# Attention: negated row maxima become rows of the query stack by two DMAs through HBM instead of by TensorE, the ring of banks and VectorE

## The reference, cut to what matters

```python
scores = jnp.einsum('bhqd,bhkd->bhqk', Q, K) * scale
attn = jax.nn.softmax(scores, axis=-1)
out = jnp.einsum('bhqk,bhkd->bhqd', attn, V)
```

## Time and profile before

| | us |
|---|---|
| median of 3 runs | 2127.63 (2123.89 to 2129.58) |
| the profiled execution | 2127.73 |
| its span in the trace | 2125.9 |
| attention in it, first scores to last | 132.79 to some 904 |
| PE busy in the span | 1809.8 (85%) |
| DVE busy | 1201.9 (57%) |
| ACT busy | 905.9 (43%) |
| POOL busy | 436.5 (21%) |
| mean granted clock of TensorE | 0.927 |

### The profile page before, as it was taken

The page is one execution under the profiler, slowest core; times in us unless marked ns, Lnnn a source line. Parts: engine busy times, 40 slices in busy tenths (PEclk is TensorE's granted clock), DMA queues, the critical chain, the costliest instruction groups (busy, mean ns, idle before and its releaser), DMA issues. The chain is left out here.

```text
span 2125.9 us, 37885 instructions
## 1 busy us (share of the span) xinstructions
PE 1809.8 (85%) x11264; PEld 1147.6 (54%) x11265; DVE 1201.9 (57%) x2635; ACT 905.9 (43%) x1362; POOL 436.5 (21%) x570
## 2 busy tenths in 40 slices
PE   7889999999999999976599999999994885067771
PEld 4423444444444444363488888888884465036551
DVE  4578888888888888644611111111113896946334
ACT  3436666666666666743033223323331520031333
POOL 2210000000000000030033333333331001202772
PEclk9969999999999999997799999999997998575996
DMA  4511111111111111054343433444442001141224
GB/s 146 187 42 35 31 34 33 30 37 30 33 34 30 37 30 32 14 166 169 138 109 95 114 113 100 107 116 112 97 112 81 1 1 60 64 158 23 48 40 161
DMA packets 103320, 159.38 MB, mean 75 GB/s; under 512 B 20704, under 2 KB 79392, under 8 KB 97760
## 3 DMA queue, kind: packets, MB, share of 16 engines
q1 hardware_dynamic: 69712, 118.46, 17.3%
q0 software_dynamic: 22656, 24.51, 6.7%
q10 hardware_dynamic: 10896, 15.73, 2.2%
HBM read 124.19 MB, written 49.02 MB: 81 GB/s over the span
## 5 line engine op out<-in xcount | busy, mean ns | idle before, releaser
L548 DVE TENSOR_REDUCE unit_max<-ps_ring 128x1 f32<-128x512 f32 x1024 | 639.6, 684 | 70.5 <-PE ps_ring L423 64.4
L534 ACT ACTIVATE w<-ps_scores 128x1024 f32<-128x1024 f32 x512 | 503.6, 1022 | 265.4 <-PE ps_scores L500 262.7
L423 PE MATMUL ps_ring<-k_stack,q_stack 96*128 96x512 bf16 x1024 | 367.5, 393 | 21.1 <-POOL v_padded L386 9.5
L500 PE MATMUL ps_scores<-q_stack,k_stack 98*128 98x512 bf16 x1024 | 307.3, 382 | 2.6 <-ACT w L534 2.5
L1513 PE MATMUL m_ps_h<-m_xt,m_w 128*128 128x256 f32 x1248 | 278.5, 382 | 0.8 <-DVE m_xt L1564 0.8
L1525 PE MATMUL m_ps_y<-w,m_ht 128*128 x1248 | 275.8, 379 | 0.0
L445 PE MATMUL ps_o<-w,v_padded 128*32 128x256 f32 x4096 | 260.8, 384 | 0.0
L1513 PEld LDWEIGHTS m_ps_h<-m_xt,m_w 128*128 128x128 f32 x1248 | 238.9, 192 | 34.1 <-DVE m_xt L1564 1.2
L1525 PEld LDWEIGHTS m_ps_y<-w,m_ht 128*128 128x128 f32 x1248 | 234.2, 190 | 30.3
L423 PEld LDWEIGHTS ps_ring<-k_stack,q_stack 96*128 96x128 bf16 x1024 | 98.7, 97 | 262.0 <-DVE unit_max L548 177.1
L1545 ACT ACTIVATE m_ht<-m_ps_h,m_w 128x256 f32<-128x256 f32 x312 | 130.7, 470 | 144.6 <-PE m_ps_h L1513 144.6
(11 more groups left out here) (244 smaller groups left out, 1860.4 us busy)
## 6 DMA issues: line engine op xcount, KB each, us to landing
m_w<-in_w SPq DMA_DIRECT2D x39, 1028.0 KB, 4.9
rows<-g_rows SPq DMA_DIRECT2D x16, 512.0 KB, 2.9
y<-sums SPq DMA_DIRECT2D x16, 512.0 KB, 7.6
q_parts<-qk_part SPq DMA_DIRECT2D x16, 384.0 KB, 3.7
k_parts<-qk_part SPq DMA_DIRECT2D x16, 384.0 KB, 3.8
q_stack<-q_parts SPq DMA_DIRECT2D x64, 96.0 KB
k_stack<-k_parts SPq DMA_DIRECT2D x64, 96.0 KB
xt<-in_xt ACTq DMA_DIRECT2D x8, 512.0 KB, 4.3
```

The lines of the kernel that those rows point to most:

```text
L423: nc.tensor.matmul(out[:, :], qs[0:STACK, u, qt * P:(qt + 1) * P], ks[0:STACK, u, half * HALF:(half + 1) * HALF], start=True, stop=True).t ...
L500: mm = nc.tensor.matmul(p_s[kt % 2][:, half * HALF:(half + 1) * HALF], ks[:, u, kt * P:(kt + 1) * P], qs[:, u, half * HALF:(half + 1) * HALF],
L534: nc.scalar.activation(pt[:, kt, :], p_s[kt % 2][:, :], ACT.Exp, scale=SCALE)\
L548: nc.vector.tensor_reduce(unit_max[:, u % 2, half, qt:qt + 1], src[:, :], axis=AX.X, op=ALU.max).then_inc(ring_used, 1)
```

## The change

`rows_unit`, `copy_rows` and the tile `neg_rows` go. SP now waits for `neg_parts` itself, writes it to a buffer in HBM (`neg_parts_out`, 128 rows of 16 two-byte elements for each slot), waits until this has landed, and reads the buffer by columns into the two rows of the slot, 1024 elements each. A third wait is new on POOL: it overwrites `neg_parts` only when the store of two heads earlier has landed. The places `rows` and `spare` leave the ring's list, so that a group has 66 places instead of 72, and the fold has one place. On SP the row step stands behind the loads, at the top of a head's turn.

```diff
@@ -273,7 +273,6 @@
-        negt = [mem.sb(f"neg_rows{u}", [MAXROWS * KT, P], BF16) for u in range(2)]
@@ -291,8 +290,10 @@
+        parts_out = mem.sem("b_parts_out")
+        neg_dram = c.neg_parts
-        FOLD_AT, ROWS_AT, COPY_AT = 4, 2, 1
+        FOLD_AT, COPY_AT = 4, 1
@@ -301,24 +302,19 @@
             for kt in range(KT):
                 if not (last and u >= 2):
                     yield kt, "max0"
-                if kt == ROWS_AT and not (last and u == SLOTS - 1):
-                    yield kt, "rows"
                 if not (last and u >= 2):
                     yield kt, "max1"
                 if kt == FOLD_AT and u % 2 == 0 and not (first and u == 0):
-                    yield kt, "spare"
                     yield kt, "fold"
-        FIRST_ROWS = 2 * KT + 4
-        PROLOGUE = 2 * 2 * KT + 1
+        PROLOGUE = 2 * 2 * KT
         def first_units():
             for at in range(PROLOGUE):
-                n = at - (at > FIRST_ROWS)
-                yield (at, None, 0, 0) if at == FIRST_ROWS else (at, n // (2 * KT), n % (2 * KT) // 2, n % 2)
-        PER_GROUP = SLOTS * (2 * KT + 1) + 2 * (SLOTS // 2)
+                yield at, at // (2 * KT), at % (2 * KT) // 2, at % 2
+        PER_GROUP = SLOTS * 2 * KT + SLOTS // 2
         assert PER_GROUP % RING == 0
         def count_before(g, first, last, u):
@@ -326,10 +322,10 @@
-            return g * PER_GROUP + (PROLOGUE - 2 + inside)
+            return g * PER_GROUP + (PROLOGUE - 1 + inside)
-            base = PROLOGUE if first else PROLOGUE - 2
+            base = PROLOGUE if first else PROLOGUE - 1
@@ -356,23 +352,26 @@
                 for u in range(3):
                     load(0, u)
-                def rows(u, at):
-
-                    sp.wait_ge(ring_used, at + 1)
+                def rows(n, u):
+
+                    sp.wait_ge(parts_done, n + 1)
+                    sp.dma_start(neg_dram[u], negp[u % 2][:, :, :].rearrange("p s t -> p (s t)"))\
+                        .then_inc(parts_out, 16)
+                    sp.wait_ge(parts_out, n * 16 + 16)
                     sp.dma_start(qs[STACK:STACK + MAXROWS, u, :].rearrange("s (t q) -> s t q", t=KT),
-                                 negt[u % 2][:, :]).then_inc(slot_loaded[u], 16)
+                                 neg_dram[u].rearrange("q (s t) -> s t q", s=MAXROWS),
+                                 allow_slow_non_contiguous=True).then_inc(slot_loaded[u], 16)
                 def body(g, first, last):
                     for u in range(SLOTS):
                         if first and u == 0:
-                            rows(0, FIRST_ROWS)
+                            rows(0, 0)
                         if not (last and u > 0):
                             wait_from(sp, scores_ready, (g * SLOTS + u) * KT)
                             load(g + (1 if u > 0 else 0), (u + 3) % SLOTS)
-                        for j, (_, kind) in enumerate(units(first, last, u)):
-                            if kind == "rows":
-                                rows((u + 1) % SLOTS, count_before(g, first, last, u) + j)
+                        if not (last and u == SLOTS - 1):
+                            rows(g * SLOTS + u + 1, (u + 1) % SLOTS)
                 groups(sp, body)
             @block.gpsimd
@@ -390,6 +389,8 @@
                     wait_apart(pool, spare_p, parts_done, n)
                     wait_apart(pool, spare_p, best_done, n + 1)
+
+                    wait_apart(pool, spare_p, parts_out, n * 16 - 16)
                     nc.gpsimd.tensor_scalar(neg[:, :], best[u % 2][:, :], -1.0, None, ALU.mult).then_inc(neg_order, 1)
                     wait_apart(pool, spare_p, neg_order, n * 2 + 1)
@@ -423,14 +424,6 @@
                     nc.tensor.matmul(out[:, :], qs[0:STACK, u, qt * P:(qt + 1) * P],
                                      ks[0:STACK, u, half * HALF:(half + 1) * HALF],
                                      start=True, stop=True).then_inc(ring_ready, 1)
-
-                def rows_unit(n, u, at, out):
-
-                    pe.wait_ge(parts_done, n + 1)
-                    claim(at)
-                    nc.tensor.transpose(out[0:MAXROWS * KT, 0:P // 2].bitcast(BF16),
-                                        negp[u % 2][:, :, :].rearrange("p s t -> p (s t)"),
-                                        c.identb[:, :]).then_inc(ring_ready, 1)
                 def pv(n, u, i):
@@ -449,19 +442,15 @@
                 def fold_unit(n, at, out):
                     pe.wait_ge(o_copied, n + 2)
-                    claim(at + 1)
+                    claim(at)
                     for blk in range(4):
                         mm = nc.tensor.transpose(out[:, blk * P:(blk + 1) * P],
                                                  o_sb[:, blk // 2, blk % 2 * P:(blk % 2 + 1) * P], c.ident[:, :])
-                        if blk >= 2:
-                            mm.then_inc(ring_ready, 1)
+                    mm.then_inc(ring_ready, 1)
                 pe.wait_ge(init, 5)
                 for at, u, qt, half in first_units():
-                    if u is None:
-                        rows_unit(0, 0, at, ring[at % RING])
-                        continue
                     if qt == 0 and half == 0:
                         pe.wait_ge(slot_loaded[u], LOADS)
@@ -479,12 +468,8 @@
-                                if kind == "rows":
-                                    rows_unit(n + 1, u + 1, at, out)
-                                elif kind == "fold":
-                                    fold_unit(n - 2, at - 1, out)
-                                elif kind == "spare":
-                                    continue
+                                if kind == "fold":
+                                    fold_unit(n - 2, at, out)
@@ -556,29 +541,19 @@
                     nc.vector.tensor_tensor(best[u % 2][:, :], unit_max[:, u % 2, 0, :], unit_max[:, u % 2, 1, :],
                                             ALU.max).then_inc(best_done, 1)
-                def copy_rows(u, at, src):
-
+                def normalise(n, pair, at, src):
                     dve.wait_ge(ring_ready, at + 1)
-                    nc.vector.tensor_copy(negt[u % 2][:, :], src[0:MAXROWS * KT, 0:P // 2].bitcast(BF16))\
-                        .then_inc(ring_used, 1)
-
-                def normalise(n, pair, at, src):
-                    dve.wait_ge(ring_ready, at + 2)
                     wait_from(dve, ring_used, at)
                     o = src[:, :].rearrange("p (m r) -> p m r", r=32)
                     nc.vector.reciprocal(rec[:, :], o[:, :, HD]).then_inc(rec_done, 1)
                     dve.wait_ge(rec_done, pair + 1)
-                    nc.vector.sem_inc(ring_used, 1)
                     nc.vector.tensor_tensor(
                         c.ao[:, bass.ds(n, 2), :, :].rearrange("p h t r -> p (h t) r"),
                         o[:, :, 0:HD], rec[:, :].unsqueeze(2).to_broadcast([P, 2 * KT, HD]),
                         ALU.mult).then_inc(ring_used, 1)
                 for at, u, qt, half in first_units():
-                    if u is None:
-                        copy_rows(0, at, ring[at % RING])
-                        continue
                     reduce_unit(u, u, qt, half, at, ring[at % RING])
                     if qt == KT - 1 and half == 1:
                         combine(u, u, at)
@@ -589,19 +564,15 @@
-                            if kind == "rows":
-                                copy_rows(u + 1, at, src)
-                            elif kind == "fold":
-                                normalise(n - 2, g * 2 + (u // 2 - 1), at - 1, src)
-                            elif kind == "spare":
-                                continue
+                            if kind == "fold":
+                                normalise(n - 2, g * 2 + (u // 2 - 1), at, src)
-                normalise(NH - 2, NH // 2 - 1, end, bank(GROUPS - 1, False, True, SLOTS, 1))
+                normalise(NH - 2, NH // 2 - 1, end, bank(GROUPS - 1, False, True, SLOTS, 0))
@@ -2159,6 +2130,7 @@
+    c.neg_parts = dram("neg_parts_out", [SLOTS, P, MAXROWS * TB], BF16)
```

4 lines of the change are left out of this document (2 added, 2 removed).

## The result

| | us |
|---|---|
| before, median of 4 runs | 2125.76 (2122.61 to 2129.58) |
| changed kernel, median of 4 runs | 3137.53 (3130.28 to 3155.85) |
| ratio | 1.479 (95% interval 1.475 to 1.482) |
| span of the profiled execution, before and after | 2125.9 and 3134.6 |

The kernel became slower by 1009 us by the spans. I had forecast 403 more, 2531 us; the result lies inside the range, at a place that I had given 20%.

A forecast was written before the change was run, and what follows sets the result against it. TensorE, with VectorE leaning on it, bounded attention at 12.11 us a head; SP's serial beat of 18.48 would replace it. 63 beats gave +401.3, the first head +9.0, missing loads -7.4: +403, 2531 us; range 2190 to 3450.

The forecast's parts named there:

- the beat: Attention's time per head, 12.11 us before the change; forecast to become 18.48 us, set by SP's work in series.
- The count: SP's column transfer from HBM into the two rows: 2048 packets on two engines, 1024 on each.
- The place of the new wait: PE's largest new wait: scores for the DMA into q_stack, about 6 us a head; ScalarE and VectorE wait for PE.
- The clock: TensorE's granted clock might fall with idle time; cost left at zero, at the 1.2 GHz level the time would be 2596 us.
- the price of a packet: Two-byte packets of the column transfer: 12.5 ns each on an engine, the middle of 8.6 and 16.3.
- my sum: SP's work from one column transfer's issue to the next: 7.37 us plus 0.868 d, together 18.48 us.
- the chain around it: SP's beat besides the hold: 1.3 us to first packet, 3.72 loads, 0.05 between jobs, 2.2 store, 0.1 wake; 7.37 us.
- slow packets: Rival for the column transfer: 26 ns a packet, d 26.6, beat 30.5, time 3300 us; 16.3 to 26 ns had 20%.
- d: Data time of the column transfer: 1024 packets on each engine at 12.5 ns, 12.8 us.
- my formula for a queue that does not hold the chain: Rival where SP is not held: beat 15.4 us, time 2344 us; 13% together with packets of 5.3 to 8.6 ns.
- The removed work: Transposes, copies and ring places taken away: some 32 us if all else stayed hidden, bounds 0 to 51; forecast worth nothing here.
- The point from which the rows are hidden: Column transfer's d at which the beat stays 12.11 us: 5.5 us, 5.3 ns a packet; the hidden case had 8%.

The follow-up runs named there:

- the slope: Changed kernel with the column transfer taking 8 of 16 columns, 1024 pieces instead of 2048: 2397.1 us, 1.130 of the kernel before; its transfer took 14.7 us against 27.6.
- apart: Changed kernel with the column transfer going to partitions 96 and 100 of a separate tile, maxima left out: 2446.9 us, 1.151 of the kernel before.
- pieces: Kernel before with single transfers ahead of it, each waited for: plain column transfer 22.3 and 26.5 us, one partition from 8 engines 13.8, 16 partitions 6.6.
- places: Kernel before with single transfers into various partitions ahead of it: 96 and 97 took 27.1 us, 96 and 100 took 15.0, 16 spread partitions 5.3.
- loads_on_act: Changed kernel with a head's six loads issued on ACT's queue instead of SP's: 3039.1 us, 1.432 of the kernel before.
- whole_rows: Changed kernel with the second transfer reading two contiguous 2 KB runs, maxima under the wrong queries: 2103.0 us, 0.991 of the kernel before.
- the strips: Changed kernel reading columns into 16 partitions, then a third transfer into the two rows: neighbouring partitions 2128.8 us (1.003), partitions 8 apart 2106.4 us (0.991).

## Why the prediction was right in its direction and wrong in its size

**Right.** What bounded the kernel, and that a step that doesn't fit into 12.11 us becomes the beat. The count: 2048 packets on two engines, to the packet. The place of the new wait: PE for the rows, with VectorE and ACT behind it, though it is some 14 us a head where I had put 6. SP's queue fills and holds it, but later than I had it: its own line of the column transfer is 0.68 us, not 10 or more, and the hold falls on the loads behind (828.30 to 838.4). The clock fell to 0.74, and the beat shows no cost of it: a head's turn took 13 us instead of 10.5, inside a beat of 28 in which PE then waits 14. The stages behind attention did not move (1230.2 and 1230.4 us from the last head's scores to the end).

**The step that failed** is the price of a packet: "the middle of 8.6 and 16.3, 12.5 ns". It measured 24 to 25 ns on each engine: 25.2 by the slope, and (26.7 - 1.8) / 1024 = 24.3 over the mean of the heads. So the data lasted 24.9 us on average instead of 12.8. A beat grew by 15.7 us beyond 12.11, where I had 6.4. In my sum the doubled term adds 0.868 x 12.1 = 10.5 us; the miss is 9.3, since the chain around it was 1.2 us too long. The rival "slow packets", 26 ns, "because a two-byte write costs more than a plain one", was the right one; its band, 16.3 to 26 ns, had 20%. Its mechanism was only half named: it is not an engine's price, but some 12 ns a piece at a place in SBUF that both engines wrote to (`apart`, `pieces`, `places`).

Both rows behind the 12.5 were readings of packets, and packets say how long an engine holds one, not when a write is done: in `pieces` 1032 of them passed in 1 us of a transfer of 13.8. That the 12.5 ns resembles the 12.6 ns that both engines together needed for a piece is luck: I meant each engine's own price. A row with the landing would have been the better bound, though before the change none had such writes. I had put the doubt into the range, where it belonged, and too little of it into the middle.

**The chain.** My sum (SP held for 0.868 d, then the six loads, then the store) reads SP's issues as the beat. They are not: the store waits behind the stream on the two engines, and the loads cost 0.8 us of a beat, not 3.7 (`loads_on_act`). With d = 24.9 the serial sum gives 7.37 + 0.868 x 24.9 = 29.0 us, my formula for a queue that does not hold the chain, d + 2.6, gives 27.5; measured 27.8. Of the size of the miss this is the smaller part, with the other sign. The store, for which I had 2.2 us, lands 4.0 us after its issue (median); issued earlier, in `loads_on_act`, it lands 10.8 us after (median), which is how a wait behind the stream looks.

One number in that step was added up wrongly: the slices 17 to 31 of the earlier trace rows sum to 5605, not 5224. That makes 145 packets on each engine instead of 135 and 0.858 of d instead of 0.868, 0.1 us a beat and 8 us in all, and the miss does not come from it.

**The removed work**, 0 to 51 us with 32 as the value if it were hidden, measured 18.6 (`whole_rows`). The point from which the rows are hidden, 5.5 us of data, agrees with the strips: a transfer of 6.6 us alone left 23.7 us of waits in all, one of 5.3 us left 2.0. They have one transfer more and other places for the loads, so this is no exact test.

**Figures of the Trainium skill.** The Trainium skill's figure (DMA: Bandwidth & Descriptors, Measured) of 10.5 ns per packet, from 4 KB in 64 packets, would have led, as an estimate, to 2417 us; the measurement decides, and for two-byte pieces in one place it was 24 to 25 ns on each engine. The Trainium skill's warning that a strided last dimension becomes one descriptor per element (DMA: Bandwidth & Descriptors, Rules for kernel authors) agrees with the count of 2048. The factor of 19 in the same table of the Trainium skill would, by my estimate of 2.4 us from it, have hidden the transfer; the transfer took 26.7 us on average.

## What to carry to other kernels

Count the pieces of a transfer and ask where each is written: the two-byte writes of this case queued at their destination, so spread such writes over partitions that are some distance apart before adding engines, and make a contiguous hop of the rest. Price such a transfer by its issue and its landing, never by its packets. And before an operation leaves a busy engine for a queue, hold the queue's latency against the beat: what was removed here was worth 0.9%, what was added cost 48%, and the same idea with the elements spread kept the 0.9%.

## What the runs showed of the hardware that I had not expected

- A two-byte write by DMA takes 10 to 13 ns at its place in SBUF, whichever engine sends it: 1024 into one partition from 8 engines 13.8 us, 2048 into 96 and 97 from two engines 22.3 to 27.1, into 96 and 100 15.0. Four-byte elements: 9.0 alone, 13.8 in the kernel.
- It is the same at 4-byte steps (26.1 us) and somewhat less at 8-byte (22.4) and at 32-byte steps (17.9). Pieces of 32 bytes at those steps: 9.1.
- The packets of such a transfer are over long before it lands: 11 us before with one partition and 8 engines, some 4 us before in the changed kernel.
- Two-byte writes into HBM took 7.5 ns each in all, from 16 engines, and no more from two (14.1 us for 2048).
- The same transfer, alone on the chip's queues, took 22.3 us once and 26.5 us right after it. That spread stays open; with the two engines on two places, in the kernel, it was 15.0 to 15.7.
